# A decoder of two layers on one core: where TensorE's instruction list has the score steps of the first two attentions

## The chip, the cores and the metric

The kernel runs on 1 core of one Trainium2 chip. The metric is device time in microseconds (us) of one launch. Engines are named as in the profile: PE is TensorE (PEld its weight loads), DVE VectorE, ACT ScalarE, POOL GpSimd, SP SyncE, which issues the DMAs.

## What is computed

A decoder with two layers on x of 16 sequences of 64 tokens of 512 features, 1024 tokens in all. Each layer is self-attention, cross-attention and a feed-forward part, each followed by adding its input and a layer norm:

```python
x = _layernorm(x + _L0_attn_ref(x, ...))     # 32 query heads, 8 key heads, width 128, causal
x = _layernorm(x + _L0_xattn_ref(x, ...))    # linear attention over the context
x = _layernorm(x + _L0_ffn_ref(x, ...))      # 4-bit weights, gated
x = _layernorm(x + _L1_attn_ref(x, ...))     # 32 query heads, 8 key heads, bias by distance, causal
x = _layernorm(x + _L1_xattn_ref(x, ...))    # 32 query heads, 8 key heads, normalised q and k
x = _layernorm(x + _L1_ffn_ref(x, ...))
```

Both self-attentions are, for each of 8 key heads and its 4 query heads:

```python
s = q @ k.T * scale + bias
out = softmax(s) @ v
y += out @ wo
```

All of it is float32. The kernel keeps this accuracy by writing a matrix as a high and a low part and adding three products.

## The kernel before

The whole model runs as one program. Each engine has its own instruction list, and the lists meet by semaphores. Three stages use the code that the change touches: `attn0` and `attn1`, the two self-attentions, and `xattn1`, the second cross-attention (`rms` is true for it alone).

A self-attention works in 8 groups, one for each key head. A group has twelve projection units `U_0` to `U_11` (keys in two halves of 512 tokens, queries of four heads in the first half of the tokens, then of four heads in the second half, then values in two halves), each a block of 12 products of 128x128 by 128x512: 4 pieces of the depth, three products each (`mm3`, lines 285 to 287). The tokens are worked in four pairs of tiles, numbered 0 to 3. Beside the units the steps of a group are, each followed by the number of its pair or tile:

- `SC`: scores, 16 small products of 128x64 (line 603), into bank 2. VectorE then does four operations on them (L881 twice: scale and bias; L887: maximum; L889: subtraction), ScalarE the exponential (L758), VectorE sum and reciprocal (`SU`, L893, L895), GpSimd the normalisation (L1036).
- `TR`: VectorE transposes the probabilities in 32x32 blocks (L901), SyncE moves them out to memory and back in the right order.
- `PT`: the transposed probabilities as high part (ScalarE, L774) and residual (VectorE, L929).
- `PV`: value products (TensorE, L646, 12 products into banks 5 and 7), then high part (ScalarE, L778) and residual (VectorE, L935), two each.
- `WO` 0 to 7: output projection of one tile of 128 tokens, a block of 12 products as large as a unit's (L285 to L287). VectorE then adds it to x (L941).
- `VT` 0 and 1: TensorE turns half of the values (L633, 4 products into bank 3), high part (ScalarE, L753) and residual (VectorE, L839).
- `WS`: output weights as high part (ScalarE, L785) and residual (VectorE, L944).

The order is written out by hand in `schedule` (line 65), as one text. Every engine goes through the same list and does its part of each step; a step that an engine has no part in is skipped. A minus behind a step means that it belongs to the group before. Two things shift steps against that list. `later` (line 98) holds a kind of step back by some events: ScalarE's exponentials by 2, VectorE's `SU` by 3. GpSimd and SyncE have orders of their own, in their `step` functions. Group 0 runs the list without the aged steps (`first_group`), groups 1 to 6 run all of it, group 7 all but `WO6-` and `WO7-`, and then comes a tail with its own list for the last products.

Banks bind some steps. `project_out` writes bank 6 for every tile and waits until VectorE has added the tile before:

```python
st.need(pe, "o_ready", 8 * i + 2 * (t // 2) + 2)
st.need(pe, "x_added", 8 * i + t - 1 if tail and t else 8 * i + t)
```

`scores` writes bank 2 and waits until VectorE has taken the scores before (`s_out`), and for the projection units of its tokens. `transpose_v` writes bank 3 and waits for the residual of the transposition before:

```python
st.need(pe, "proj_free", 12 * i + 11 + n)
st.need(pe, "v_ready", 2 * i + n)
```

In SyncE's list `load_bias` of `attn1` waits for all four `s_out` of its group, and the load of the value weights (chunk 5) comes behind it. In GpSimd's list the split of chunk 5 (L1019, L1021) stands ahead of the normalisation of pair 2.

Of the kernel before, what the change touches and what calls it, by code (L numbers as in the profile page):

```python
# [54 lines left out]
def events(text):  # L55

    out = []
    for word in text.split():
        age = word.count("-")
        word = word.rstrip("-")  # L60
        out.append((word[:2], int(word[2:]), age))
    return out


def schedule(rms, project, attend):

    if rms:  # L70
        ev = events("WS0- WS1- PT0- U_0 SS3- WS2- WS3- U_1 PV0- PT1- U_2 SC2- SD2- EX2- U_3 SU2- WO0- TR2- PV1- SC3- SD3- EX3- "
                    "U_4 KT0 SU3- WO1- U_5 KT1 TR3- PT2- SQ0 U_6 PV2- SS0 U_7 WO2- PT3- SQ1 WO3- SS1 PV3- WO4- SC0 SD0 EX0 "
                    "WO5- SU0 SC1 SD1 EX1 U_8 TR0 SU1 U_9 TR1 SQ2 WO6- U_10 SS2 U_11 SQ3 WO7-")
    else:
        ev = events("U_0 VT1- PT0- TR2- U_1 WS0- WS1- U_2 PV0- PT1- TR3- WS2- WS3- U_3 WO0- PV1- U_4 PT2- WO1- U_5 PV2- WO2- SC0 "
                    "PT3- WO3- SC1 U_6 PV3- WO4- U_7 WO5- U_8 TR0 WO6- U_9 TR1 WO7- SC2 U_10 SC3 U_11 VT0")
    if not project:
        if rms:
            return events("PT0- PV0- WO6-- SS3- PT1- WO7-- WS0- WS1- SC2- SD2- WS2- WS3- EX2- SU2- PV1- SC3- TR2- WO0- SD3- EX3- "
                          "SU3- WO1- TR3- WO2- PT2- WO3- PV2- WO4- PT3- WO5- PV3- WO6- WO7-")  # L80
        return events("PT0- TR2- WO6-- VT1- PV0- PT1- TR3- WO7-- WS0- WS1- PV1- WS2- WS3- WO0- PT2- WO1- "
                      "PV2- WO2- PT3- WO3- PV3- WO4- WO5- WO6- WO7-")
    if project == "last":
        return [e for e in ev if e[0] != "WO" or e[1] < 6]
    return [e for e in ev if attend or not e[2]]


def first_group(rms, tensor):

    if not rms:  # L90
        return schedule(False, True, False)
    if tensor:
        return events("U_0 U_1 U_2 U_3 U_4 KT0 U_5 KT1 U_6 SS0 U_7 U_8 SC0 SS1 U_9 SC1 U_10 U_11 SS2")
    return events("U_0 U_1 U_2 U_3 U_4 KT0 U_5 KT1 SQ0 U_6 SS0 U_7 SQ1 SS1 SD0 EX0 SU0 SD1 TR0 U_8 U_9 SQ2 EX1 SU1 TR1 "
                  "U_10 U_11 SS2 SQ3")
# [17 lines left out]
def program(nc, a):  # L113
    with ExitStack() as ctx:
# [478 lines left out]
        def pe_attention(pe, st):  # L593
# [89 lines left out]
            if st.name == "attn1":  # L683
                pe.wait_ge(const_set, 2)
                pe.wait_ge(xt_ready, 8 * 2)
            run(0, first_group(st.rms, True))
            run(1, schedule(st.rms, True, True))
            with pe.Fori(2, NKV - 1) as i:
                run(i, schedule(st.rms, True, True))
# [1486 lines left out]
```

## Time and profile before

| | us |
|---|---|
| median of 3 runs | 2276.7 (2272.69 to 2279.4) |
| the profiled execution | 2275.88 |
| its span | 2274.1 |

| engine | busy us | share |
|---|---|---|
| TensorE, products | 2141.0 | 94% |
| TensorE, weight loads | 1726.2 | 76% |
| VectorE | 1340.2 | 59% |
| GpSimd | 811.5 | 36% |
| ScalarE | 801.6 | 35% |

The first self-attention is the first 565 us or so, the second lies between about 1055 and 1620. A group takes about 67.6 us. Products are pipelined: a 512-column product is shown as 0.39 us long, while the next starts 0.23 us after it. So what a step costs TensorE is read from start to start.

### The profile page before, as it was taken

To read this page: it belongs to the slowest core of one execution; us is meant where nothing else is said; L and a number is where in the kernel's file an instruction comes from. 1 tells how busy PE (TensorE), PEld (TensorE's weight loads), DVE (VectorE), ACT (ScalarE), POOL (GpSimd) and SP (SyncE) were. 2 spreads that over 40 slices of the span, in tenths; PEclk is the share of its full clock that TensorE was granted. 3 is DMA by queue.
4 is the path that set the end of the run, shared out by engine and by line. 5 is a ranking of instruction groups with operands and counts; after the bars stand their busy time and mean duration, and the time that the engine had idled before them with its cause. 6 is when DMAs were issued, how large, how long until landed. Compare 5 with 4: busy or idle time off the path is not lost.

```text
span 2274.1 us, 33829 instructions
## 1 busy us (share of the span) xinstructions
PE 2141.0 (94%) x11763; PEld 1726.2 (76%) x11763; DVE 1340.2 (59%) x2243; ACT 801.6 (35%) x1524; POOL 811.5 (36%) x759
## 2 busy tenths in 40 slices
PE   8999999998899978888999999999989999999978
PEld 6888888886566566666788888887778888888867
DVE  3454444457898736565444445445686676766665
ACT  2332222232777625552322233222233333333321
POOL 4221222212455446665222222220454333434233
PEclk9999999999999989998999999999999999999999
DMA  5222212212000221211222222322232212222120
GB/s 168 65 67 83 83 51 69 70 37 80 15 24 18 83 72 38 93 37 57 85 63 61 78 61 75 84 59 55 61 83 62 65 52 72 70 68 60 31 77 38
DMA packets 119051, 146.30 MB, mean 64 GB/s; under 512 B 16192, under 2 KB 68016, under 8 KB 118448
## 3 DMA queue, kind: packets, MB, share of 16 engines
q1 hardware_dynamic: 118960, 145.10, 22.1%
q8 instruction: 56, 0.92, 0.2%
q14 instruction: 35, 0.29, 0.0%
HBM read 117.78 MB, written 27.26 MB: 64 GB/s over the span
## 4 chain that ended last, share of the span: by engine, by line
PE 78%; DVE 7%; POOL 6%; issue 5%; ACT 2%; DMA 1%; SPq 0%; POOLq 0%; DVEq 0%; ACTq 0%
PE banks L285 20%; PE banks L287 18%; PE banks L286 18%; PE banks L603 7%; PE banks L646 3%; POOL f_t L1807 2%; PE banks L1250 1%; PE banks L1257 1%; PE banks L1220 1%; PE banks L1267 1%; PE banks L1286 1%; PE banks L1236 1%; PE banks L1614 1%; POOL f_il L1795 1%; PE banks L1615 1%
## 5 line engine op out<-in xcount | busy, mean ns | idle before, releaser
L285 PE MATMUL banks<-xTh,wh 128*128 128x512 f32 x1024 | 418.8, 409 | 12.9 <-DVE xTl L2057 8.7
L287 PE MATMUL banks<-xTh,wl 128*128 128x512 f32 x1024 | 404.9, 395 | 0.0
L286 PE MATMUL banks<-xTl,wh 128*128 128x512 f32 x1024 | 403.6, 394 | 0.0
L285 PE MATMUL banks<-woh,oth 128*128 128x512 f32 x768 | 313.1, 408 | 16.2 <-DVE X L941 7.0
L287 PE MATMUL banks<-woh,otl 128*128 128x512 f32 x768 | 301.6, 393 | 0.0
L286 PE MATMUL banks<-wol,oth 128*128 128x512 f32 x768 | 301.5, 393 | 0.0
L1036 POOL TENSOR_TENSOR sc_sb<-sc_sb,rs 128x512 f32<-128x512 f32 x96 | 103.7, 1083 | 554.1 <-DVE rs L895 554.1
L941 DVE TENSOR_TENSOR X<-banks,X 128x512 f32<-128x512 f32 x192 | 132.2, 689 | 275.7 <-PE banks L287 274.9
L738 ACT ACTIVATE q_sb<-banks 128x512 f32<-128x512 f32 x192 | 114.5, 596 | 402.3 <-PE banks L287 402.3
L285 PEld LDWEIGHTS banks<-xTh,wh 128*128 128x128 f32 x1024 | 195.5, 191 | 54.6 <-issue 9.2
L287 PEld LDWEIGHTS banks<-xTh,wl 128*128 128x128 f32 x1024 | 194.9, 190 | 43.8
L286 PEld LDWEIGHTS banks<-xTl,wh 128*128 128x128 f32 x1024 | 195.5, 191 | 37.0
L1019 POOL TENSOR_SCALAR wh<-raw 128x512 fp32r<-128x512 f32 x144 | 93.6, 650 | 343.7 <-DMA raw<-in_a_in 184.4
L1021 POOL TENSOR_TENSOR wl<-raw,wh 128x512 fp32r<-128x512 f32 x144 | 194.8, 1353 | 12.0
L935 DVE TENSOR_TENSOR otl<-banks,oth 128x512 fp32r<-128x512 f32 x192 | 123.5, 685 | 128.0 <-ACT oth L778 128.0
L603 PEld LDWEIGHTS banks<-k_sb,q_sb 128*128 128x128 f32 x1536 | 185.7, 193 | 16.4 <-ACT q_sb L738 6.7
L603 PE MATMUL banks<-k_sb,q_sb 128*128 128x64 f32 x1536 | 184.7, 274 | 6.5 <-ACT q_sb L738 4.1
L285 PEld LDWEIGHTS banks<-woh,oth 128*128 128x128 f32 x768 | 145.4, 189 | 59.2 <-DVE wol L944 8.1
L287 PEld LDWEIGHTS banks<-woh,otl 128*128 128x128 f32 x768 | 145.3, 189 | 32.1
L286 PEld LDWEIGHTS banks<-wol,oth 128*128 128x128 f32 x768 | 145.8, 190 | 26.6
L778 ACT ACTIVATE oth<-banks 128x512 fp32r<-128x512 f32 x192 | 104.3, 596 | 137.7 <-PE banks L646 137.7
L758 ACT ACTIVATE sc_sb<-sc_sb 128x512 f32<-128x512 f32 x96 | 60.4, 631 | 225.3 <-DVE sc_sb L889 225.3
(231 smaller groups left out, 3951.2 us busy)
## 6 DMA issues: line engine op xcount, KB each, us to landing
raw<-in_a_in SPq DMA_DIRECT2D x144, 256.0 KB, 2.8
raw<-in_a_out SPq DMA_DIRECT2D x96, 256.0 KB, 2.8
turned<-pq SPq DMA_DIRECT2D x384, 64.0 KB, 1.8
pt<-turned SPq DMA_DIRECT2D x96, 256.0 KB, 2.8
f_q<-in_f_q SPq DMA_DIRECT2D x21, 512.0 KB, 4.0
f_s<-in_f_s SPq DMA_DIRECT2D x9, 512.0 KB, 5.5
X<-in_x SPq DMA_DIRECT2D x1, 2048.0 KB, 11.3
x_craw<-in_ctx SPq DMA_DIRECT2D x8, 256.0 KB, 2.7
```

What stands on the lines that cost most here:

```text
L285: nc.tensor.matmul(out, w_hi, x_hi, start=start, stop=False)
L286: nc.tensor.matmul(out, w_hi, x_lo, start=False, stop=False)
L287: return nc.tensor.matmul(out, w_lo, x_hi, start=False, stop=stop)
L603: last = nc.tensor.matmul(pb[2][:, (4 * c + m) * S:(4 * c + m + 1) * S], q_sb[:, 4 * (pair % 2) + m, c * P:(c + 1) * P], k_sb[:, col:col + S],
L646: last = nc.tensor.matmul(PVB[b][:, cols], v_part[r, 2 * pair + t, :], by_query[p_part][r, t], start=v_part is vh and p_part == 0, stop=v_ ...
L738: nc.scalar.activation(q_sb[:, :, g * S:(g + 1) * S], bank[:, :].rearrange("p (c s) -> p c s", c=8), ACT.Copy).then_inc(A["q_free" if st.r ...
L778: nc.scalar.activation(oth[:, n % 2, :, 64 * b:64 * b + 64], PVB[b][:, :].rearrange("p (c s) -> p c s", c=8), ACT.Copy).then_inc(A["o_hi"], 1)
L935: nc.vector.tensor_tensor(otl[:, n % 2, :, half], PVB[b][:, :].rearrange("p (c s) -> p c s", c=8), f32(oth[:, n % 2, :, half]), ALU.subtra ...
L941: nc.vector.tensor_tensor(xtile(n), bank[:, :], xtile(n), ALU.add).then_inc(A["x_added"], 1)
L1019: nc.gpsimd.tensor_scalar(hi, src, 1.0, 0.0, ALU.mult, ALU.add).then_inc(A["w_hi"], 1)
L1021: nc.gpsimd.tensor_tensor(lo, src, f32(hi), ALU.subtract).then_inc(A["w_ready"], 1)
L1036: nc.gpsimd.tensor_tensor(rows, rows, spread_rows(rs[:, pair, :]), ALU.mult).then_inc(A["p_ready"], 1)
```

## The change

In the list of the self-attentions three score steps change their places. Nothing else is edited.

```diff
     else:
-        ev = events("U_0 VT1- PT0- TR2- U_1 WS0- WS1- U_2 PV0- PT1- TR3- WS2- WS3- U_3 WO0- PV1- U_4 PT2- WO1- U_5 PV2- WO2- SC0 "
-                    "PT3- WO3- SC1 U_6 PV3- WO4- U_7 WO5- U_8 TR0 WO6- U_9 TR1 WO7- SC2 U_10 SC3 U_11 VT0")
+        ev = events("U_0 VT1- PT0- TR2- U_1 WS0- WS1- U_2 PV0- PT1- TR3- WS2- WS3- U_3 WO0- PV1- U_4 PT2- WO1- U_5 PV2- SC0 WO2- "
+                    "PT3- WO3- PV3- SC1 U_6 WO4- U_7 WO5- U_8 TR0 WO6- U_9 TR1 WO7- SC2 U_10 U_11 SC3 VT0")
```

`SC0` comes ahead of `WO2-` instead of behind it. `PV3-` comes ahead of `U_6` instead of behind it, with `SC1` between the two. `SC3` comes behind `U_11` instead of ahead of it. As the list is everyone's, VectorE's and ScalarE's orders move with it: VectorE's becomes PV2, SC0, WO2, PT3, WO3, SU0, PV3, SC1, WO4, SU1 in the middle of the group and SC2, SC3, SU2, VT0, SU3 at its end, the latter as before.

## Rows read from the trace of the kernel before

**Rows 1.** Chain shares; one group's us busy: PE, PEld, DVE, ACT, POOL; clock, DMA.

```profile
PE 78%; DVE 7%; POOL 6%; issue 5%; ACT 2%; DMA 1%; SPq 0%; POOLq 0%; DVEq 0%; ACTq 0%
...
339.00:406.00 67.00, 66.80 (x359) 55.08 (x358) 31.25 (x54) 18.10 (x34) 15.94 (x16) 1.00 0.24 67
```

**Rows 2.** TensorE's timeline (start us, us, what), attn1: two blocks touching.

```profile
1220.95 0.39 PE L285 MATMUL banks<-woh,oth 128*128 128x512 f32 x1
...
1223.67 0.39 PE L285 MATMUL banks<-xTh,wh 128*128 128x512 f32 x1
```

**Rows 3.** The same, attn0: starts of PV2, WO2, SC0, WO3, SC1's follower, PV3.

```profile
353.04 0.39 PE L646 MATMUL banks<-pth,vh 64*128 64x256 f32 x2
...
353.95 0.50 PE L285 MATMUL banks<-woh,oth 128*128 128x512 f32 x1
...
356.81 1.89 PE L603 MATMUL banks<-k_sb,q_sb 128*128 128x64 f32 x16
...
358.51 0.48 PE L285 MATMUL banks<-woh,oth 128*128 128x512 f32 x1
...
363.06 0.48 PE L285 MATMUL banks<-xTh,wh 128*128 128x512 f32 x1
...
366.00 0.39 PE L646 MATMUL banks<-pth,vh 64*128 64x256 f32 x2
```

**Rows 4.** The same, end of the group: SC3, VT0, VT1.

```profile
390.64 1.89 PE L603 MATMUL banks<-k_sb,q_sb 128*128 128x64 f32 x16
...
395.20 0.60 PE L633 MATMUL banks<-ident,vst 128*128 128x128 f32 x4
...
398.41 0.60 PE L633 MATMUL banks<-ident,vst 128*128 128x128 f32 x4
```

**Rows 5.** The same, xattn1: scores directly behind value products.

```profile
1758.86 2.00 PE L603 MATMUL banks<-k_sb,q_sb 128*128 128x64 f32 x16
```

**Rows 6.** The same: last product of WO2, first of WO3, VectorE's addition.

```profile
1780.75 0.39 PE L287 MATMUL banks<-woh,otl 128*128 128x512 f32 x1
...
1781.92 0.50 PE L285 MATMUL banks<-woh,oth 128*128 128x512 f32 x1 [0.78 <-DVE X L941]
...
1781.17 0.69 DVE L941 TENSOR_TENSOR X<-banks,X 128x512 f32<-128x512 f32 x1 [4.08 <-PE banks L287]
```

**Rows 7.** VectorE's timeline, attn0: PV2's residual, SC0's first, its follower.

```profile
354.69 1.29 DVE L935 TENSOR_TENSOR otl<-banks,oth 128x512 fp32r<-128x512 f32 x2 [3.58 <-ACT oth L778]
...
358.73 0.76 DVE L881 SCALAR_TENSOR_TENSOR sc_sb<-banks,bias 128x256 f32<-128x256 f32 x2 [1.04 <-PE banks L603]
...
360.86 0.68 DVE L929 TENSOR_TENSOR ptl<-pt,pth 128x512 fp32r<-128x512 f32 x1
```

**Rows 8.** ScalarE's timeline, attn0: the copy of U_5's queries.

```profile
353.14 0.60 ACT L738 ACTIVATE q_sb<-banks 128x512 f32<-128x512 f32 x1 [4.32 <-PE banks L287]
```

**Rows 9.** VectorE's timeline, attn0, group 7: SU2, VT0's residual, PT0's residual.

```profile
526.90 0.69 DVE L893 TENSOR_REDUCE ssum<-sc_sb 128x8 f32<-128x512 f32 x1 [1.77 <-ACT sc_sb L758]
...
527.74 0.64 DVE L839 TENSOR_TENSOR vl<-banks,vh 128x512 fp32r<-128x512 f32 x1
...
529.13 0.64 DVE L929 TENSOR_TENSOR ptl<-pt,pth 128x512 fp32r<-128x512 f32 x1
```

**Rows 10.** TensorE's timeline, attn0, group 7: SC3.

```profile
520.99 1.89 PE L603 MATMUL banks<-k_sb,q_sb 128*128 128x64 f32 x16
```

**Rows 11.** Timelines, attn1, group's end: VectorE at SC3, GpSimd at chunk 5.

```profile
1241.04 0.76 DVE L881 SCALAR_TENSOR_TENSOR sc_sb<-banks,bias 128x256 f32<-128x256 f32 x2 [2.35 <-PE banks L603]
...
1246.31 0.62 POOL L1019 TENSOR_SCALAR wh<-raw 128x512 fp32r<-128x512 f32 x1 [12.12 <-DMA raw<-in_a_in]
```

**Rows 12.** Busy by window as in rows 1: group 0, xattn1 twice.

```profile
28.00:40.00 12.00, 10.99 (x50) 9.66 (x51) 4.27 (x8) 0.60 (x1) 0.00 (x0) 0.72 0.08 23
...
1757.00:1764.00 7.00, 7.00 (x50) 5.86 (x49) 5.78 (x10) 1.15 (x3) 6.27 (x7) 1.00 0.26 48
...
1778.00:1785.00 7.00, 6.18 (x27) 4.43 (x25) 3.67 (x5) 1.60 (x3) 0.81 (x1) 1.00 0.00 1
```

## Prediction

> **What bounds the kernel now.** I read three views, in this order. First the chain that ended last: TensorE has 78% of it, the rest is spread thin [rows 1]. Then the busy times of one head group of a self-attention: 66.80 of 67 us of TensorE, under half of that on any other engine, granted clock 1.00, which is the 2.4 GHz level [rows 1]. Then TensorE's own timeline. There each product starts where the one before it stops occupying the array, so distance from start to start is what a step costs, and the printed durations, which overlap, are not. So the time of these stages is TensorE's instruction stream plus each wait that TensorE has to sit out. In groups 1 to 7 as they stand it sits out next to none. VectorE's idle time is its cover.
>
> Prices from the timeline, start to start:
> - A block of twelve 512-column products behind another such block: 1223.67 − 1220.95 = 2.72 us [rows 2].
> - The same block behind a small step: 356.81 − 353.95 = 2.86 behind value products [rows 3]. Behind scores, with one score step: 363.06 − 358.51 = 4.55, and the score step alone is 358.51 − 356.81 = 1.70, so 2.85. A change to a small step and back thus costs some 0.13 us of refill.
> - Value products: 353.95 − 353.04 = 0.91, with another 0.09 ahead of them (366.00 − 363.06 = 2.94 against 2.85) [rows 3].
> - Value transposition: 398.41 − 395.20 = 3.21, less a block of 2.86, gives 0.35 [rows 4].
> - Scores directly behind value products are in the trace only in the cross-attention: that step is 2.00 long instead of 1.89 [rows 3, 5]. I take 1.70 + 0.11 = 1.81 us.
>
> **First edit: SC0 ahead of WO2, PV3 and SC1 together.** Nothing is added or removed. TensorE's order from the third value product on was PV2, WO2, SC0, WO3, SC1, U_6, PV3, WO4. It becomes PV2, SC0, WO2, WO3, PV3, SC1, U_6, WO4. By starts, the old order takes 366.00 − 353.04 = 12.96 to the start of PV3, plus 0.91 and 2.86 for PV3 and WO4: 16.73 us [rows 3].
>
> What counts is that WO2 and WO3 now touch. Both write bank 6 (`wo_bank`), and `project_out` makes TensorE wait for `x_added`, VectorE's addition of the product before. SC0's 1.70 us stood between them and covered that addition. The trace shows what it costs bare. In the cross-attention these same two, WO2 and WO3, touch: the last product of WO2 starts at 1780.75, the addition at 1781.17, the next block at 1781.92 [rows 6]. That is 1.17 us instead of the 0.23 (2.72 / 12) between two products, a stall of 0.94, and behind it a refilled block of 2.86.
>
> Is VectorE free in time? Its order changes with TensorE's: the residual of PV2, then SC0's four operations, then WO2's addition. From PV2's start as zero: residual 1.65 to 2.94 (354.69 − 353.04, 1.29 long) [rows 3, 7]; SC0 from about 2.94 (score step from 0.91, 2.00 long); its four operations hold the engine for 360.86 − 358.73 = 2.13 [rows 7], so to about 5.1. WO2's product runs from 2.72 to 5.57 and its output is there near 5.74. So VectorE waits, and the stall stays at 0.94. SC0 also needs the queries of U_5: ScalarE's copy runs from 353.14 to 353.74 and SC0 would begin at 353.95, so it is ready with 0.2 us to spare [rows 3, 8].
>
> The new order: PV2 0.91, SC0 1.81, WO2 2.85, stall 0.94, WO3 2.86, step to PV3 0.09, PV3 0.91, SC1 1.81, U_6 2.86, WO4 2.72 = 17.76 us. Difference 17.76 − 16.73 = +1.03 us. Without the stall the WO3 block is clean as well, 0.94 + 0.14 less, and the difference is −0.05: the regrouping saves about what the dearer scores cost. PV3 now comes earlier, right after WO3. Its probabilities need VectorE's residual (PT3), which stands right behind WO2's addition and so runs inside WO3: free. The first scores' exponentials and sums (EX, SU0) stay ahead of their use, and SU1 moves about 1 us later, as TensorE does. GpSimd's two normalisations follow SU0 and SU1, and what they lead to, TR0 and TR1, stands behind U_8 and U_9, one block and more behind SU1. This edit counts in groups 1 to 7 of two stages. Group 0 has no aged steps, and its SC0 and SC1 touch before and after. 14 × 1.03 = 14.4 us.
>
> **Second edit: SC3 behind U_11.** The old order is SC3, U_11, VT0, U_0, VT1. The new one is U_11, SC3, VT0, U_0, VT1. From SC3's start to VT1's start the old one takes 398.41 − 390.64 = 7.77 [rows 4]. VT1 writes the bank that VT0 used and needs VectorE's residual of VT0 (`v_ready`). On VectorE that residual stands behind SC3's four operations and SU2. In the old order there were two 2.8 us blocks for that; now there is one. VectorE's chain from SC3's start: first operation at 358.73 − 356.81 = 1.92 [rows 3, 7]; the four hold it 2.13; SU2 until the residual is 527.74 − 526.90 = 0.84; the residual 0.64 [rows 9]; and 0.06 to TensorE's restart (1781.92 less the end of the addition at 1781.86) [rows 6]. Sum 5.59. TensorE itself would be there at 1.70 + 0.35 + 2.86 = 4.91, so it stalls 0.68. Ahead of SC3, U_11 now follows U_10 as a clean block of 2.72. New: 2.72 + 5.59 = 8.31; old 7.77; +0.54 us. The trace shows no scores ahead of a transposition: if that passage is dearer, it lies inside the stall and costs nothing; if cheaper, likewise. Fourteen times: 7.6 us. The eighth time in each stage is group 7, where the tail follows. There VectorE works without a gap: SC3 starts at 520.99 and the next residual that TensorE waits for, PT0's, at 529.13, 8.14 later [rows 9, 10]. New: 2.72 + 1.92 + 2.13 + 0.84 + 1.39 (529.13 − 527.74, the value residual and SU3) = 9.00. So +0.86, twice: 1.7 us. If the tail absorbs it, this term is 0.
>
> SyncE is touched too. In the second self-attention the next bias load waits for SC3's `s_out`, and the value weights' load (chunk 5) waits in SyncE's queue behind it. GpSimd splits chunk 5 before it normalises pair 2, and TR2 on VectorE waits for that. The split now starts 5.27 us behind SC3's first operation (1246.31 − 1241.04) [rows 11], so 7.2 behind SC3's start, ends some 2 us later, and pair 2 is normalised by 10.4. TR2 then ends by 11.1 and two residuals of WS by 12.4. The next thing that TensorE needs of VectorE behind these is the residual of PV0, whose input is there 13.2 after SC3's start (VT1 5.59, its 0.35, blocks 2.86 and 2.72, 0.09, then 1.65). Cover 0.8 us. If it fails, up to 0.5 us a group in this stage.
>
> **Sum.** 14.4 + 7.6 + 1.7 = +23.7 us. The profiled execution took 2275.88, its span 2274.1, with 1.8 around it. It lies 0.8 under the median of the runs shown, 2276.7. So 2299.6 from the profiled execution, 2300.4 by the median. I give 2300.
>
> One rule speaks against even this sum. In the rows, the bare wait of TensorE in the cross-attention leaves the clock at 1.00 [rows 12], and by them the sum stands. The Trainium skill, "TensorE: Matmul & The Clock Gate", section "A second HAM failure mode: psum-queue depth-cycling", says that short idle times of TensorE between groups of products can be frequent enough for its clock to fall back and rise again. By that rule the time is the first rival's.
>
> **The rivals.**
> - *The clock falls at each new cluster.* In group 0 of the first stage two score steps and the gaps of 0.7 and 1.0 us around them were followed by the 1.2 GHz level: the stretch has a mean granted clock of 0.72 [rows 12]. That is 12 × 0.28 = 3.4 us lost. In each of 14 groups it would be 14 × 3.4 = 47 us more: 2347. Against it: the cross-attention has value products and scores side by side (clock 1.00) and the bare WO wait (clock 1.00) [rows 12], each by itself, which is what a new group has. 3%.
> - *Both waits are hidden.* If the addition of WO2 and the residual of VT0 reached TensorE before it arrived, only the order of the blocks is left: 14 × (−0.05) and 16 × (2.72 + 4.91 − 7.77 = −0.14), in all −2.9: 2273. This is the case that is not slower. It decides from the point at which VectorE's 0.69 us addition ends within the 0.23 us between two products, and no row has that; the cross-attention's row has the opposite. 4%.
> - *Only the second stall is hidden*, because VectorE's chain from SC3 is shorter than I stacked it. 14.4 − 16 × 0.14 = +12: 2288. VectorE would need to be 0.7 us faster over five operations that the trace times; 7%.
> - *A cover fails besides*: SC0's operations run past WO2's end (0.6 us in hand), or the second stage's late normalisation blocks VectorE, or GpSimd beside VectorE lengthens the chain. 14 × 0.6 = +8 more: 2308 to 2313. 12%.
> - *The change does not do what it says*: the order of VectorE and ScalarE comes from the same list through `later`, so one of them could be unmoved. The list of TensorE decides, and it moves. Time as before, 2276: 1%.
>
> **How the numbers follow.** Forecast 73%, alone between 2294 and 2306 (stall 0.88 to 1.0, scores behind value products 1.70 to 1.9, tail 0 to 1.7). The range reaches down near the third rival, up over the fourth: 2291 to 2311, which leaves out the clock, the hidden waits, most of the third rival and the outer half of the fourth, near 2 in 10. A measurement of this kernel tells about 0.3%, 7 us, from no change. Slower by more: 73 + 3 + 7 + 12 = 95, less what I keep for something unseen: 92%. Within: the hidden waits and the unmoved order, 6%. Faster by more: 2%.
>
> **What would show it.** In the profile after, TensorE's idle rows should show 14 of about 0.8 us before a WO block released by the addition at L941, and about 14 before a value transposition (L633) released by the residual at L839. Scores behind value products should be 2.00 long. The clock in the groups should be 1.00. If the first kind is absent, the central step is wrong; if the second is absent, the chain from SC3 was mis-stacked; a clock below 1.00 in groups 1 to 7 would make it much slower.

## The result, and the profile after

Four runs of the changed kernel have a median of 2306.31 us (2304.43 to 2307.84), four of the kernel before beside them 2274.88 (2272.69 to 2279.4). The ratio is 1.0135, with a 95% interval of 1.0123 to 1.0147: slower by 1.35%, some 31 us. The forecast was 2300, the range 2291 to 2311; as a difference it was +23.7 us. One of the four executions of experiment e3 below took 2548 us at a mean granted clock of 0.80 and is left out of that experiment's ratio.

The profiled execution took 2306.99 us, its span 2305.2, which is 31.1 more than before. The page of the kernel after, its busy times (share of the span) and instructions, and the shares of the chain:

```profile
PE 2149.3 (93%) x11763; PEld 1727.0 (75%) x11763; DVE 1343.3 (58%) x2243; ACT 807.2 (35%) x1524; POOL 812.1 (35%) x759
...
PE 77%; DVE 10%; POOL 5%; issue 5%; ACT 2%; DMA 0%; POOLq 0%; DVEq 0%; SPq 0%; ACTq 0%
```

TensorE's busy time has grown by 8 us only (overlaps are counted once, so less overlap shows as more), VectorE's by 3, so most of the 31 us is idle time of TensorE. In the chain VectorE has gone from 7% to 10% [rows 1]. The groups of instructions by line say which waits came. Behind the second bar stands the idle time ahead of these instructions, then what ended most of it. First the kernel before, then after:

```profile
L285 PE MATMUL banks<-woh,oth 128*128 128x512 f32 x768 | 313.1, 408 | 16.2 <-DVE X L941 7.0 <-DVE otl L935 5.8 <-DVE wol L944 3.2
...
L944 DVE TENSOR_TENSOR wol<-raw,woh 128x512 fp32r<-128x512 f32 x96 | 68.9, 758 | 21.6 <-ACT woh L785 21.6
```

```profile
L285 PE MATMUL banks<-woh,oth 128*128 128x512 f32 x768 | 312.8, 407 | 30.2 <-DVE X L941 18.3 <-DVE wol L944 6.1 <-DVE otl L935 5.8
...
L633 PE MATMUL banks<-ident,vst 128*128 128x128 f32 x128 | 20.1, 279 | 9.3 <-DVE vl L839 9.3
...
L944 DVE TENSOR_TENSOR wol<-raw,woh 128x512 fp32r<-128x512 f32 x96 | 73.9, 809 | 17.3 <-ACT woh L785 17.3
```

Ahead of the first products of a `WO` block the idle time went from 16.2 to 30.2 us, 11.3 more by VectorE's addition at L941 and 2.9 more by the residual of the output weights at L944. Ahead of the value transpositions (L633) it went from 0.0 to 9.3. The two predicted waits are there and a third beside them. The mean of L944 rose from 758 to 809 ns, though nothing about this operation was edited.

A group from `SC0` to the next `SC0` took 67.6 us before in both stages (67.57 to 67.75, the last one 67.26), 69.25 after in `attn0` and 69.8 in `attn1`. These, and the lengths of groups below, are medians of the groups 1 to 6 in the profiled execution.

**The first edit in the trace.** TensorE's timeline of the kernel after in `attn0` (start, duration, what; in brackets idle time before it and what ended it), PV2, SC0, WO2, WO3, PV3, SC1, U_6:

```profile
360.36 0.39 PE L646 MATMUL banks<-pth,vh 64*128 64x256 f32 x2
...
361.27 2.00 PE L603 MATMUL banks<-k_sb,q_sb 128*128 128x64 f32 x16
363.08 0.48 PE L285 MATMUL banks<-woh,oth 128*128 128x512 f32 x1
...
366.88 0.50 PE L285 MATMUL banks<-woh,oth 128*128 128x512 f32 x1 [0.78 <-DVE X L941]
...
369.84 0.39 PE L646 MATMUL banks<-pth,vh 64*128 64x256 f32 x2
...
370.75 2.00 PE L603 MATMUL banks<-k_sb,q_sb 128*128 128x64 f32 x16
372.56 0.48 PE L285 MATMUL banks<-xTh,wh 128*128 128x512 f32 x1
```

From PV2's start to the end of WO4 is 378.13 (the start of U_7) less 360.36, 17.77 us where the sum said 17.76. WO3 starts 3.80 behind WO2 instead of 2.86, a stall of 0.94, with 0.78 of idle time shown. That is the row of the cross-attention [rows 6], to the hundredth. Scores behind value products are 2.00 long and cost 1.81. VectorE's timeline beside it: the residual of PV2, SC0's first operation, WO2's addition.

```profile
362.02 1.29 DVE L935 TENSOR_TENSOR otl<-banks,oth 128x512 fp32r<-128x512 f32 x2 [3.58 <-ACT oth L778]
363.31 0.76 DVE L881 SCALAR_TENSOR_TENSOR sc_sb<-banks,bias 128x256 f32<-128x256 f32 x2
...
366.13 0.69 DVE L941 TENSOR_TENSOR X<-banks,X 128x512 f32<-128x512 f32 x1 [0.62 <-PE banks L287]
```

The addition had waited 0.62 us for TensorE's last product, so VectorE was early, as predicted, and the time is the bare passage from TensorE to VectorE and back. There are 14 such waits, seven in each stage, of 0.78 or 0.88.

**The second edit in the trace.** TensorE, `attn0`, from U_11 on: U_11, SC3, VT0, U_0, VT1, U_1. Below them VectorE: SU2, the residual of VT0.

```profile
399.01 0.39 PE L285 MATMUL banks<-xTh,wh 128*128 128x512 f32 x1
...
401.73 1.89 PE L603 MATMUL banks<-k_sb,q_sb 128*128 128x64 f32 x16
403.46 0.61 PE L633 MATMUL banks<-ident,vst 128*128 128x128 f32 x4
403.82 0.47 PE L285 MATMUL banks<-xTh,wh 128*128 128x512 f32 x1
...
407.34 0.66 PE L633 MATMUL banks<-ident,vst 128*128 128x128 f32 x4 [0.51 <-DVE vl L839]
407.75 0.48 PE L285 MATMUL banks<-xTh,wh 128*128 128x512 f32 x1
...
405.78 0.68 DVE L893 TENSOR_REDUCE ssum<-sc_sb 128x8 f32<-128x512 f32 x1
...
406.61 0.67 DVE L839 TENSOR_TENSOR vl<-banks,vh 128x512 fp32r<-128x512 f32 x1
```

SC3 to VT1 is 5.61 where the sum said 5.59, and the residual ends at 407.28, 0.06 ahead of the transposition that needs it. One number was missing: behind that wait the transposition costs 0.41 rather than 0.35. In `attn0` 1.57 us a group were predicted (1.03 and 0.54) and 1.64 measured.

**What was too small.** `attn1` is the same but for its bias, and its group is 0.54 us longer. The rows of the kernel after, in order of engine (SyncE's loads, GpSimd, VectorE, TensorE), where group 3 of `attn1` begins:

```profile
1261.11 1.29 SPq L482 DMA_DIRECT2D bias<-in_alibi  x2
1262.65 0.38 SPq L468 DMA_DIRECT2D raw<-in_a_in  x1
...
1270.76 0.92 SPq L468 DMA_DIRECT2D raw<-in_a_in  x2
...
1265.71 0.62 POOL L1019 TENSOR_SCALAR wh<-raw 128x512 fp32r<-128x512 f32 x1 [15.09 <-DMA raw<-in_a_in]
...
1267.98 2.04 POOL L1036 TENSOR_TENSOR sc_sb<-sc_sb,rs 128x512 f32<-128x512 f32 x2
1273.74 0.62 POOL L1019 TENSOR_SCALAR wh<-raw 128x512 fp32r<-128x512 f32 x1 [3.72 <-DMA raw<-in_a_in]
1274.45 1.59 POOL L1021 TENSOR_TENSOR wl<-raw,wh 128x512 fp32r<-128x512 f32 x1
...
1269.16 0.71 DVE L901 STREAM_TRANSPOSE pq<-sc_sb 128x512 f32<-128x512 f32 x1 [2.29 <-POOL sc_sb L1036]
1269.79 1.39 DVE L944 TENSOR_TENSOR wol<-raw,woh 128x512 fp32r<-128x512 f32 x2
1271.59 1.29 DVE L935 TENSOR_TENSOR otl<-banks,oth 128x512 fp32r<-128x512 f32 x2 [0.41 <-ACT oth L778]
...
1274.02 2.57 DVE L944 TENSOR_TENSOR wol<-raw,woh 128x512 fp32r<-128x512 f32 x2
...
1273.70 0.39 PE L285 MATMUL banks<-woh,oth 128*128 128x512 f32 x1
...
1276.65 0.50 PE L285 MATMUL banks<-woh,oth 128*128 128x512 f32 x1 [0.72 <-DVE wol L944]
...
1277.54 0.39 PE L646 MATMUL banks<-pth,vh 64*128 64x256 f32 x2
```

The same place in `attn0`, where group 6 begins (SyncE's load of chunk 0, GpSimd's split of it, VectorE's second pair of residuals):

```profile
412.81 0.91 SPq L468 DMA_DIRECT2D raw<-in_a_in  x2
...
416.44 1.66 POOL L1021 TENSOR_TENSOR wl<-raw,wh 128x512 fp32r<-128x512 f32 x1
...
417.49 1.76 DVE L944 TENSOR_TENSOR wol<-raw,woh 128x512 fp32r<-128x512 f32 x2
```

Read downwards in `attn1`: the bias load waits for SC3's `s_out`, chunk 5's load stands behind it, GpSimd's split begins at 1265.71, and pair 2 is normalised late, so `TR2` waits 2.29 us on VectorE. It starts 10.9 behind SC3 (1258.25), where 10.4 was predicted. The first two residuals of the output weights then run, then PV0's, which is in time. The cover of 0.8 us that the prediction named held, and VectorE's second pair of residuals starts 15.8 behind SC3 in both stages (SC3 is at 401.73 in `attn0`). So VectorE has caught up. What has not is a load. SyncE brings the next group's chunk 0 into the slot that the first residual of the output weights leaves free, so it waits for that residual (`wo_ready`). The load is issued 12.5 behind SC3 instead of 11.1, and GpSimd's L1021 on it starts 16.2 behind SC3 instead of 14.7. In `attn0` it holds up the second pair by some half a microsecond: the pair takes 1.76 us, where alone it takes 1.25. In `attn1` it meets the last residual in full: the pair takes 2.57, and 2.35 to 2.44 in the five other groups that have it. WO0, which started at 1273.70, stands still for 0.72 us ahead of its last weight tile. WO0 costs 3.84 instead of the 3.13 that the same place had before; in the other five groups it is 3.62 to 3.72. The six together are 3.3 us.

The Trainium skill, "SBUF — State Buffer", section "Who interferes with whom", says that a VectorE instruction with two SBUF inputs contends with a GpSimd instruction that reads SBUF, and calls the port pair that the two engines share an exclusive lock. The trace agrees: the second of the pair, due to start at about 1274.7, ended at 1276.59, which is 0.55 behind the end of GpSimd's L1021 (1274.45 + 1.59 = 1276.04). The same meeting was in the kernel before, in groups 1 to 6 of both stages, where it could be seen and wasn't:

```profile
407.48 1.64 POOL L1021 TENSOR_TENSOR wl<-raw,wh 128x512 fp32r<-128x512 f32 x1
...
408.51 1.75 DVE L944 TENSOR_TENSOR wol<-raw,woh 128x512 fp32r<-128x512 f32 x2
```

### The profile page after: what moved, and what is told of

The parts are those of the page before. It is cut to its first block, busy times and chain, and to the rows that moved or that the text cites. A ratio compares the mean times of both kernels' runs of the same rounds, so it can differ in the third digit from the quotient of the medians.

```text
span 2305.2 us, 33829 instructions
## 1 busy us (share of the span) xinstructions
PE 2149.3 (93%) x11763; PEld 1727.0 (75%) x11763; DVE 1343.3 (58%) x2243; ACT 807.2 (35%) x1524; POOL 812.1 (35%) x759
## 4 chain that ended last, share of the span: by engine, by line
PE 77%; DVE 10%; POOL 5%; issue 5%; ACT 2%; DMA 0%; POOLq 0%; DVEq 0%; SPq 0%; ACTq 0%
PE banks L285 19%; PE banks L287 18%; PE banks L286 18%; PE banks L603 7%; PE banks L646 3%; POOL f_t L1807 2%; PE banks L1250 1%; PE banks L1257 1%; PE banks L1220 1%; PE banks L1267 1%; PE banks L1286 1%; PE banks L1236 1%; DVE X L941 1%; PE banks L1614 1%; POOL f_il L1795 1%
## 5 line engine op out<-in xcount | busy, mean ns | idle before, releaser
L285 PE MATMUL banks<-woh,oth 128*128 128x512 f32 x768 | 312.8, 407 | 30.2 <-DVE X L941 18.3
L941 DVE TENSOR_TENSOR X<-banks,X 128x512 f32<-128x512 f32 x192 | 132.2, 688 | 338.3 <-PE banks L287 337.7
L1021 POOL TENSOR_TENSOR wl<-raw,wh 128x512 fp32r<-128x512 f32 x144 | 197.1, 1369 | 12.0
L881 DVE SCALAR_TENSOR_TENSOR sc_sb<-banks,bias 128x256 f32<-128x256 f32 x128 | 48.4, 419 | 147.4 <-PE banks L603 131.1
```

Of the source, the lines that this page charges most:

```text
L285: nc.tensor.matmul(out, w_hi, x_hi, start=start, stop=False)
L941: nc.vector.tensor_tensor(xtile(n), bank[:, :], xtile(n), ALU.add).then_inc(A["x_added"], 1)
L1021: nc.gpsimd.tensor_tensor(lo, src, f32(hi), ALU.subtract).then_inc(A["w_ready"], 1)
```

## Experiments

Each is named by its label. "After" and "before" are the two kernels. Ratios are to the kernel before, measured beside it on the same chip; after has 1.0135.

### The two edits apart

e1 is after with the second edit undone; e2 is before with the second edit alone.

```diff
# e1, against after
-... SC2 U_10 U_11 SC3 VT0
+... SC2 U_10 SC3 U_11 VT0
# e2, against before
-... SC2 U_10 SC3 U_11 VT0
+... SC2 U_10 U_11 SC3 VT0
```

> The first edit alone (SC0 ahead of WO2, PV3 and SC1 together; SC3 stays ahead of U_11). Theory (the bare addition between WO2 and WO3 is the price): 14 idle times of TensorE near 0.8 us before WO3, none before VT1, and none before WO0 in the second self-attention; +1.03 us a group, 14 x 1.03 = +14 us on the kernel before, ratio 1.0063. Rival (the waits before WO0 in the second self-attention of the changed kernel also come from this edit): about 5 us more, ratio 1.0085, with these waits in the trace.

> The second edit alone (SC3 behind U_11). Theory (VectorE's chain from SC3 holds VT1; and in the second self-attention late scores push the chunk 5 load, the normalisation of pair 2, TR2 and WS behind each other): 16 idle times near 0.5 us before VT1, 6 before WO0 in the second self-attention, +0.54 us a group in the first self-attention, +1.3 in the second, with the tails +15 us, ratio 1.0065. Rival (the waits before WO0 need both edits): no idle times before WO0, +9 us, ratio 1.0041.

Measured: e1 1.0065 (1.0048 to 1.0081), e2 1.0065 (1.0048 to 1.0082). The sum is 1.0130, so they add up, and neither of the two edits is free. The waits separate by name. In the rows of e1 (first) and e2 (second) for the same two groups of instructions as above:

```profile
L285 PE MATMUL banks<-woh,oth 128*128 128x512 f32 x768 | 311.9, 406 | 27.9 <-DVE X L941 18.3 <-DVE otl L935 5.8 <-DVE wol L944 3.6
L633 PE MATMUL banks<-ident,vst 128*128 128x128 f32 x128 | 19.1, 271 | 0.0
```

```profile
L285 PE MATMUL banks<-woh,oth 128*128 128x512 f32 x768 | 313.5, 408 | 18.9 <-DVE X L941 7.0 <-DVE wol L944 6.0 <-DVE otl L935 5.8
L633 PE MATMUL banks<-ident,vst 128*128 128x128 f32 x128 | 20.0, 279 | 8.5 <-DVE vl L839 8.5
```

The waits for the addition (18.3, before 7.0) belong to the first edit alone, those for the value residual (8.5) to the second alone, and the third kind, for L944 (6.0, before 3.2; 3.6 in e1), nearly all to the second. By the ratio each is +14.8 us (e1 10.9 to 18.4, e2 10.9 to 18.6): the first as predicted (14.4), the second 5.5 above its 9.3. The group of e2 was 68.19 in `attn0` (+0.58 where 0.54 was predicted) and 68.73 in `attn1` (+1.1). So what the groups show of the excess stands in `attn1`.

### Is the shared bank the cause of the first wait?

e3 is after with WO3 of the self-attentions in bank 3. Then WO3 needs only the addition of WO1, and VT0, which also writes bank 3, needs WO3's addition, long done.

```diff
-    st.need(pe, "x_added", 8 * i + t - 1 if tail and t else 8 * i + t)
+    own = not st.rms and not tail and t == 3
+    st.need(pe, "x_added", 8 * i + t - 1 if (tail and t) or own else 8 * i + t)
-    bank = wo_bank(t, tail)
+    bank = own_bank(st, t, tail)      # 3 for t == 3, else as before
# transpose_v, n == 0
+    st.need(pe, "x_added", 8 * (i - 1) + 4)
```

> The changed kernel, but the self-attentions' WO3 writes bank 3 instead of bank 6 in groups 1 to 7, so that it needs not wait for VectorE's addition of WO2 (VT0 waits for the addition of WO3, which is long done). Theory: the 14 idle times before WO3 vanish and its block is clean, 14 x (0.94 + 0.14) = 15 us less than the changed kernel: ratio to the kernel before 1.0068. Rival (VectorE's time, not the bank, holds TensorE there, so the wait moves to PV3 or WO4): gain under 5 us, ratio above 1.011, and new idle times at PV3 or WO4.

Measured: 1.0057 (1.0037 to 1.0077). No row of TensorE in groups 1 to 7 waits for L941 any more, and the group takes 68.18 in `attn0` and 68.72 in `attn1`, the lengths of e2's (68.19 and 68.73). The whole cost of the first edit was the shared bank; without it the new order costs what the old did, near the −0.05 of the prediction.

### Is VectorE's order the cause of the second?

e4 is after with SU2 behind VT0's residual on VectorE.

```diff
-    return later(both, ("SU",), 3)
+    out = later(both, ("SU",), 3)
+    for a in range(len(out) - 1):
+        if out[a][:2] == ("SU", 2) and out[a + 1][:2] == ("VT", 0):
+            out[a], out[a + 1] = out[a + 1], out[a]
+    return out
```

> The changed kernel, but on VectorE SU2 (sum and reciprocal of the third scores) stands behind the residual of VT0 instead of ahead of it. Theory: the residual comes 0.84 us earlier, more than the wait of 0.68, so the idle times before VT1 vanish in groups 0 to 6: 14 x 0.68 = 9.5 us less than the changed kernel, ratio 1.009; but in the second self-attention, where TensorE's wait before WO0 hangs on VectorE's TR2, a part of this can come back there as a longer wait, so down to 5 us less, ratio 1.011. Rival (the wait before VT1 hangs on ScalarE's copy or on the transposition itself): no change to the changed kernel, ratio 1.0135.

Measured: 1.0081 (1.0064 to 1.0098). The waits ahead of the value transpositions are gone but for one of 0.80 in the first group (L633 has 0.8 us in all instead of 9.3), and the group takes 68.5 in both stages. The swap gains more than the wait itself: the `attn1` waits ahead of WO0 go with it, but for one. There VectorE's second pair of residuals follows TensorE and starts 15.2 behind SC3 instead of 15.8, while GpSimd's L1021 on chunk 0 starts at 16.4 (16.2 in after), so the pair takes 1.67 us instead of 2.35 or more. The price is in the tail, where PV0 waits for its residual at L929 1.75 us instead of 0.67. There VectorE is the late one, and SU2 stands in its way.

### The third wait: the late load, or GpSimd beside VectorE?

e5 is after with SyncE's load of chunk 5 ahead of the bias load. e8 is after with GpSimd's split of chunk 0 behind the normalisation of pair 0.

```diff
# e5, SyncE's step
-    load_bias(i + 1)
     st.need(sp, "w_ready", 6 * (i + 1) + 5)
     load_w(i + 1, 5, 4)
+    load_bias(i + 1)
# e8, GpSimd's step
-    if more:
-        pool_split_chunk(pool, st, i + 1, 0)
     normalise(i, 0)
     if more:
+        pool_split_chunk(pool, st, i + 1, 0)
         pool_split_chunk(pool, st, i + 1, 1)
```

> The changed kernel, but SyncE issues the value weights' load (chunk 5) ahead of the bias load of the next group, which waits for the late fourth scores. Theory (the waits before WO0 in the second self-attention come from that queue: late load, late split, late normalisation of pair 2, late TR2 and WS on VectorE): TR2 no longer waits for GpSimd and the six waits before WO0 vanish, 6 x 0.7 = 4 us less than the changed kernel, ratio to the kernel before 1.0117. Rival (what costs is that GpSimd's split of chunk 0 and VectorE's last residual of the output weights exclude each other, and an earlier split hits the third residual instead): TR2 is early but waits before WO0 stay, ratio 1.0135.

> The changed kernel, but in the self-attentions GpSimd splits chunk 0 of the next group behind the normalisation of pair 0, so well behind the residuals of the output weights. The fourth scores and TR2 stay late. Theory (exclusion of VectorE's two-input residual and GpSimd's split is what lengthens the last residual from 0.69 to 1.78 us and holds WO0): the residuals take 0.69 us each and the six waits before WO0 vanish, 4 us less than the changed kernel, ratio 1.0117. Rival (the late TR2 alone pushes the residuals past WO0): the waits stay at 0.5 us or more, ratio 1.0135.

Measured: e5 1.0123 (1.0105 to 1.0142), which holds both expectations and decides nothing. e8 1.0089 (1.0074 to 1.0105), below both. The rows say more. First e5 in the place shown above: VectorE's first pair of residuals, GpSimd's L1021 on chunk 0, VectorE's second pair. Then e8: VectorE's first pair, and its group of L944.

```profile
1271.14 1.29 DVE L944 TENSOR_TENSOR wol<-raw,woh 128x512 fp32r<-128x512 f32 x2 [1.37 <-ACT woh L785]
...
1275.54 1.76 POOL L1021 TENSOR_TENSOR wl<-raw,wh 128x512 fp32r<-128x512 f32 x1
...
1276.69 1.75 DVE L944 TENSOR_TENSOR wol<-raw,woh 128x512 fp32r<-128x512 f32 x2
```

```profile
1268.35 1.25 DVE L944 TENSOR_TENSOR wol<-raw,woh 128x512 fp32r<-128x512 f32 x2
...
L944 DVE TENSOR_TENSOR wol<-raw,woh 128x512 fp32r<-128x512 f32 x96 | 63.5, 701 | 16.5 <-ACT woh L785 16.5
```

In e5 the normalisation is in time and `TR2` waits no more. The load of chunk 0 goes out 11.1 behind SC3 (1260.92), L1021 starts at 14.6 behind it, and the pair at 15.8 as ever. One wait is left in `attn1` instead of six, and its group takes 69.27 instead of 69.8, the length that it has in `attn0` (69.25 after). But the second pair still meets the split (1.75 us for the pair), and a group of `attn0` is no shorter. In one group of e5's `attn0` L1021 happens to start 15.8 behind SC3, and there the pair takes 2.35 us and TensorE waits 0.53: the lateness counts in either stage. In e8 the pair takes 1.25 us, the mean of L944 falls from 809 to 701 ns over the whole kernel, and the group takes 68.93 in both stages. That is 0.86 less in `attn1` and 0.32 less in `attn0`. So the late load brought GpSimd's next split to the wrong moment; what stopped TensorE was the exclusion. Both have to be there: in e5 the lateness is gone, in e8 the partner. My expectation of e8 counted `attn1`'s waits alone and left out that `attn0` had paid too, in silence: there TensorE's step ahead of the third of the four weight tiles of WO0 was 0.40 instead of 0.23 even before, with no idle time printed.

e10 tests that on the kernel before, with the same edit.

> The kernel before, with GpSimd's split of chunk 0 behind the normalisation of pair 0 in the self-attentions, nothing else. Theory (the exclusion of GpSimd's split and VectorE's last residual of the output weights costs the kernel before too: there the pair of residuals took 1.75 us instead of 1.29 and WO0 paused 0.17 us with a refill of 0.13): 14 x 0.3 = 4 us less than the kernel before, ratio 0.998, and the pairs of residuals take 1.25 to 1.29 us. Rival (that exclusion is peculiar to the changed kernel): ratio 1.000.

Measured: 0.9986 (0.9977 to 0.9995), group 67.26 instead of 67.6 in both stages. So 3.2 us of this cost (1.1 to 5.2) were in the kernel before; by twelve groups of 0.35 it is 4.2.

### One half of the first edit

e6 is before with PV3 and SC1 ahead of U_6 and SC0 left where it was.

```diff
-... WO2- SC0 PT3- WO3- SC1 U_6 PV3- WO4- ...
+... WO2- SC0 PT3- WO3- PV3- SC1 U_6 WO4- ...
```

> The kernel before with the harmless half of the first edit alone: PV3 and SC1 together behind WO3, SC0 stays between WO2 and WO3. Theory (only the touching of WO2 and WO3 costs): no idle times before WO3, 14 x (16.71 - 16.73 us) = -0.3 us, ratio 1.000. Rival (bringing the fourth value products forward costs by itself, because VectorE or ScalarE has its probabilities too late): waits before PV3 and a ratio above 1.003.

Measured: 1.0019 (1.001 to 1.0028). The expected 1.000 is just outside, and so is the rival's 1.003, though its waits are there. TensorE's row of the first value product of PV3, e6:

```profile
360.94 0.39 PE L646 MATMUL banks<-pth,vh 64*128 64x256 f32 x2 [0.15 <-DVE ptl L929]
```

It waits 0.15 in `attn0` and 0.25 in `attn1` for its probabilities, since SC0's four operations stand ahead of PT3's residual on VectorE. In after SC0 is one block earlier and this wait isn't there. The halves of the first edit are therefore not independent: moving SC0 early uncovers the bank and covers PV3.

### All together, and a version that beats both

e7 is after with the edits of e3, e4 and e5. e11 is after with those of e3, e4 (not in group 7) and e8, and with SC3 ahead of U_11 in group 7. e12 is e11 without the first edit and bank 3, so the second edit with VectorE's and GpSimd's orders mended.

> The changed kernel with all three cures: WO3 in bank 3, SU2 behind the residual of VT0, chunk 5's load ahead of the bias load. Theory (the stalls were all that the change cost, what is left is the saved refills): 14 x (-0.05) and 16 x (-0.14), the tails some 2 us longer because VectorE works without a gap there: between -3 and 0 us on the kernel before, ratio 0.9987 to 1.000. Rival (grouped small steps cost something by themselves): ratio above 1.002.

> The changed kernel with WO3 in bank 3, SU2 behind the residual of VT0, GpSimd's split of chunk 0 behind the normalisation of pair 0, and in group 7 SC3 and SU2 where they were before, since VectorE has no slack in the tail. Theory (all stalls gone, the refills saved): 14 x (-0.3) for the exclusion, 14 x (-0.05) and 14 x (-0.14) for the order: -7 us on the kernel before, ratio 0.997. Rival (the regrouping saves nothing, only the moved split does): -4 us, ratio 0.998.

> The same as the run before it but without the first edit and without bank 3: SC0, SC1 and PV3 are where the kernel before has them. Theory: 14 x (-0.3) and 14 x (-0.14) = -6 us, ratio 0.9973, next to nothing behind the run with the first edit. Rival (the first edit without its stall is worth more than 0.05 us a group): more than 2 us behind it.

Measured: e7 1.0004 (0.9995 to 1.0013), e11 0.9968 (0.9956 to 0.998), e12 0.997 (0.9959 to 0.9981). The three mends of e7 give back all of the 1.35% and no more; its group is 67.45 long, and its tail has the 1.75 us wait of e4. e11 gains 7 us on before. The windows of after, then of e11 (busy times of PE, PEld, DVE, ACT, POOL, then granted clock and DMA), one stretch of `attn0` each:

```profile
340.00:410.00 70.00, 68.70 (x365) 56.14 (x364) 32.36 (x57) 19.17 (x34) 16.09 (x16) 1.00 0.25 67
```

```profile
339.00:406.00 67.00, 67.00 (x362) 55.66 (x362) 31.60 (x54) 19.07 (x34) 15.60 (x16) 1.00 0.25 70
```

In e11 TensorE is busy for 67.00 of 67 us. By their times e11 and e12 can't be told from each other. By their groups, 67.11 and 67.16 in both stages, the order of the first edit with the bank free brings the 0.05 us a group that the prediction gave it. Of e12's gain e10 alone has about half (3.2 of 6.8 us); the group of e12 is 67.16 long where e10 has 67.26, 0.10 a group where the prediction gave the second edit with its wait hidden 0.14, and some 1.4 us in 14 groups. The rest was not taken apart, and lies within the intervals.

## Why the prediction was right, and where it was off

The two waits that it named are there, with the causes that it gave, and the total lies in its range. But it said +23.7 us and the spans differ by 31.1. In the balance below, the missing 7.4 us are 3.3 of late splits in `attn1`, some 0.8 of the transposition behind a wait, 1.6 of clock in one tail and 1.5 in stages that the change doesn't touch. That the time still lies in the range is owed to the room left above for the fourth rival, which named a neighbour of what came, so luck has a part in it.

- **First edit: right in kind and size.** 17.77 us for 17.76, 14 waits, cause shown by e3, total agreed by e1 (14.8 for 14.4). It rested on a place in another stage of the same kernel where the two blocks already touched.
- **The regrouping as such, −0.05: right** (e11 against e12, 67.11 and 67.16; e3 against e2 shows −0.01). But a half of it alone is not free (e6), which the prediction did not weigh.
- **Second edit in `attn0`: right, 0.06 a group too small.** The chain was 5.61 for 5.59; the transposition behind a wait is 0.06 dearer. e4 showed that VectorE's order is the cause.
- **Second edit in `attn1`: under-sized, by 0.60 us a group, 0.06 of it as in `attn0`.** The step that failed is the one on SyncE's queue. It followed the late normalisation correctly (10.9 for 10.4) up to PV0's residual, found 0.8 us of cover, which held, and stopped. It didn't follow what the late first residual of the output weights releases: the load of the next chunk 0, GpSimd's split of it 1.5 us later against VectorE's second pair, and the price of that pair beside the split, 2.35 to 2.57 us where 1.75 were paid before. The fourth rival has GpSimd beside VectorE and the late normalisation in it, but not this meeting. Its size for this stage, up to 0.5 us a group, was about right: six waits with their refills, 3.3 us.
- **Tails: right, +1.7 predicted and measured.** From the first value product of PV0 inside group 7 to that of PV0 in the tail, after is 1.94 us longer than before in `attn0` and 1.93 in `attn1`. e1, with the first edit alone, is 1.07 and 1.09 longer there, and e2, with the second alone, 0.86 and 0.85, where 0.86 was predicted.
- **The clock.** It stayed at 1.00, the 2.4 GHz level, in every group after the first: the window 340 to 410 of after shows it with one of each predicted wait inside (70 less 68.70 busy is their 0.78 and 0.51). The first rival did not come true there, nor did the rule cited for it. In the tail of `attn1`, though, one stretch of after fell, where before the same work was at full clock. Windows of after, then of before, columns as above:

```profile
1609.00:1612.00 3.00, 2.60 (x16) 2.13 (x17) 3.00 (x7) 1.68 (x4) 0.96 (x1) 0.72 0.33 68
```

```profile
1581.00:1584.00 3.00, 2.58 (x19) 2.13 (x20) 3.00 (x6) 1.91 (x4) 0.98 (x1) 1.00 0.33 68
```

and TensorE's product behind which it fell, of after:

```profile
1610.40 0.77 PE L285 MATMUL banks<-woh,oth 128*128 128x512 f32 x1 [0.29 <-DVE X L941]
```

Ahead of it TensorE had stood still for 0.57, 0.67 and 0.29 us within 3 us. The block that it begins takes 4.49 us, from 1610.40 to PV1 at 1614.89, where before it takes 2.92 (1582.42 to 1585.34); most of its products start 0.43 us apart instead of 0.23, with no idle time between them. That is 1.57 us, all that this tail is longer by from there to PV3. The same three waits stand at the same distances in the tail of `attn0` (541.19, 542.48, 543.77) and in both tails of e2, e3, e5 and e8, and the clock stayed at 1.00 behind all of these. e4 and e7 have a stretch at a lower granted clock in one of their tails too. And the cross-attention of the kernel before, whose rows spoke against the first rival, has one such stretch: 0.50 from 1920 to 1922, behind 1.38 us of idle time. Each was seen in one execution, and no run was made to provoke it, so the cause stays open.

The balance by the two spans: 12.4 us at the start of `attn1`, 15.6 from there to the first WO7 of its tail, where 11.9 were predicted for each stage, and 1.6 in the rest of the tail, together 29.6 of 31.1. The last 1.5 lie in stages that the change doesn't touch, in single executions.

## What to carry to other kernels

A product block that looks like it merely stands between two others may be the cover of a handover (here 0.94 us for a bank that VectorE has to empty); before it is moved, find a place in the trace where the same pair touches, and read the price there. When an order slips on one engine, follow the slip through every operation behind it until one has waited anyway, follow too what each of them releases on the other engines (here a load), and look beside each for a partner that shuts it out. Here both engine-to-engine waits that the new order brought in could be covered, one by a free bank and one by another edit of the order, so such edits have to be timed together, not each by itself.

## What the runs showed of the hardware

- The handover of a bank from TensorE through VectorE's addition (0.69 us) and back left TensorE idle for 0.78 to 0.88 us in 14 places, the same as in the cross-attention. It did not depend on how long VectorE had been waiting.
- VectorE's residual with two SBUF inputs takes some 0.65 us alone; beside GpSimd's L1021 one ended 1.9 us behind the end of the one before it. Moving one GpSimd operation behind another was worth 10 us in after and 3 us in before by the ratios, 7 and 4 by the lengths of the groups. A part of that never showed as idle time of TensorE, only as a step of 0.40 us between two products where 0.23 is usual.
- Fourteen groups with two or three waits of 0.5 to 0.9 us each left TensorE's granted clock at 1.00. Three waits close together in a tail were followed by 0.72 in `attn1` of after, and by 1.00 in the nine other tails that have the same three.
